# A new table of turns for a two-layer decoder kernel: every block of every stage gets a start of its own

## The reference, cut to what matters

```python
x = x + L0_attn(layernorm(x))        # Mamba-2: projection, causal conv, SSD scan in one chunk of 64, gate, projection
x = x + L0_xattn(layernorm(x), ctx)  # 16 heads over 64 context rows, with rotary tables on the keys
x = x + L0_ffn(layernorm(x))         # mixture of 7 experts, top 2, and a shared expert
x = x + L1_attn(layernorm(x))        # RWKV time mixing: scans with a running maximum
x = x + L1_xattn(layernorm(x), ctx)  # 32 query heads, 8 key/value heads, no projections
x = x + L1_ffn(layernorm(x))         # 64 small experts, top 8 by softmax, mapped by inv_map
```

## Time and profile before

| | |
|---|---|
| runs | 2320.09, 2321.63, 2322.1 us; median 2321.63 |
| profiled execution | 2316.73 us, of which the span is 2314.9 |
| busy | PE 2104.8 us (91%), DVE 1378.1 (60%), ACT 1003.4 (43%), POOL 687.6 (30%) |
| granted TensorE clock, mean | 0.957 |
| chain that ended last | PE 69%, DVE 14%, issue 7%, POOL 5%, DMA 2%, ACT 2% |

### The profile page before, as it was taken

The page is one execution under the profiler, slowest core; times in us unless marked ns, Lnnn a source line. Parts: engine busy times, 40 slices in busy tenths (PEclk is TensorE's granted clock), DMA queues, the critical chain, the costliest instruction groups (busy, mean ns, idle before and its releaser), DMA issues.

```text
span 2314.9 us, 37392 instructions
## 1 busy us (share of the span) xinstructions
PE 2104.8 (91%) x13552; PEld 1608.1 (69%) x13552; DVE 1378.1 (60%) x3477; ACT 1003.4 (43%) x1984; POOL 687.6 (30%) x1056
## 2 busy tenths in 40 slices
PE   5999999999999778999994569999999999999998
PEld 4888888888888556777772346666666666666655
DVE  3367777767766431233334567777777777777631
ACT  1245555555554322333331234455545445454542
POOL 1133333433433145111113333333332333323200
PEclk9799999999999879999997579999999999999999
DMA  6200050000000054222222000000000000000000
GB/s 192 72 3 21 8 176 24 8 17 24 8 8 15 5 186 143 62 69 73 70 69 105 10 19 24 24 24 24 22 24 24 24 24 24 24 24 24 15 5 7
DMA packets 80882, 99.67 MB, mean 43 GB/s; under 512 B 17976, under 2 KB 67008, under 8 KB 80192
## 3 DMA queue, kind: packets, MB, share of 16 engines
q1 hardware_dynamic: 74560, 80.49, 11.0%
q0 software_dynamic: 6144, 16.79, 2.2%
HBM read 62.12 MB, written 35.13 MB: 42 GB/s over the span
## 4 chain that ended last, share of the span: by engine, by line
PE 69%; DVE 14%; issue 7%; POOL 5%; DMA 2%; ACT 2%; SPq 0%; ACTq 0%; POOLq 0%; DVEq 0%
PE ps L1900 11%; PE ps L1315 8%; PE ps L348 6%; PE ps L748 5%; PE ps L707 5%; PE ps L1923 4%; PE ps L1906 3%; PE ps L718 3%; POOL rows_by_slot L1159 3%; PE ps L739 2%; PE ps L397 2%; DVE arena L1703 2%; DVE arena L1461 1%; PE ps L729 1%; PE ps L374 1%
## 5 line engine op out<-in xcount | busy, mean ns | idle before, releaser
L1900 PE MATMUL ps<-BIG,arena 128*128 128x352 f32 x512 | 166.9, 469 | 5.6 <-DVE arena L1990 5.6
L1900 PE MATMUL ps<-BIG,EARLY 128*128 128x352 f32 x512 | 165.9, 467 | 6.5 <-DVE EARLY L1990 6.5
L1315 PE MATMUL ps<-BIG,arena 128*128 x648 | 149.6, 383 | 13.7 <-POOL arena L1376 13.7
L348 PE MATMUL ps<-arena,EARLY 128*128 128x256 f32 x640 | 159.0, 393 | 0.7 <-DVE arena L450 0.7
L1349 DVE COPY arena<-ps 128x256 f32<-128x256 f32 x162 | 68.8, 424 | 137.1 <-PE ps L1315 137.1
L1315 PEld LDWEIGHTS ps<-BIG,arena 128*128 128x128 f32 x648 | 121.1, 190 | 34.8 <-issue 19.3
L1900 PEld LDWEIGHTS ps<-BIG,EARLY 128*128 128x128 f32 x512 | 92.8, 190 | 60.9 <-DVE EARLY L1990 12.2
L1900 PEld LDWEIGHTS ps<-BIG,arena 128*128 128x128 f32 x512 | 93.5, 191 | 59.2 <-DVE arena L1990 11.2
L348 PEld LDWEIGHTS ps<-arena,EARLY 128*128 128x128 f32 x640 | 121.0, 195 | 19.2 <-issue 2.9
L1367 ACT ACTIVATE arena<-ps,BIG 128x128 f32<-128x128 f32 x216 | 61.9, 369 | 117.7 <-PE ps L1306 106.3
L552 POOL TENSOR_TENSOR arena<-arena 128x512 f32<-128x512 f32 x32 | 40.6, 1270 | 242.1 <-DVE arena L477 242.1
(11 more groups left out here) (408 smaller groups left out, 5164.0 us busy)
## 6 DMA issues: line engine op xcount, KB each, us to landing
rows_by_slot<-zrow SPq DMA_DIRECT2D x5, 1792.0 KB, 15.4
arena<-rows_by_slot SPq DMA_DIRECT2D x54, 128.0 KB, 2.1
results_by_slot<-arena SPq DMA_DIRECT2D x54, 128.0 KB, 1.7
BIG<-in_moe_w SPq DMA_DIRECT2D x3, 1792.0 KB, 12.4
X<-in_x SPq DMA_DIRECT2D x8, 512.0 KB, 4.3
rows_by_token<-BIG SPq DMA_DIRECT2D x16, 256.0 KB, 2.2
EARLY<-rows_by_token SPq DMA_DIRECT2D x4, 1024.0 KB, 5.5
arena<-in_ka SPq DMA_DIRECT2D x16, 256.0 KB, 2.7
```

The costliest lines, as they stand in the source:

```text
L348: m = e.matmul(ps[:, f * 256:f * 256 + 256], w_in[:, c, c0 + f * P:c0 + f * P + P], L.hT[:, c, :], start=c == 0, stop=c == 1, skip_group_c ...
L1315: m = e.matmul(ps[:, 0:256], src[q][:, c * P:c * P + P], BIG[:, bass.ds(pe_reg[2 * n + q] + (w0 + c * 256), 256)], start=c == 0, stop=c == ...
L1900: e.matmul(ps[:, 0:352], L.hT[:, q, ts], WG[:, q, gs], start=q == 0, stop=False, skip_group_check=True)
```

## The change

Only the table changes: START gets a number for every block (before, blocks of a stage stood at one distance), and all of TURNS is new. No instruction is added or taken away, and no generator, wait, tile or ring is touched. `weave` now writes the same pieces in other orders: of the keys sorted, 986 of TensorE's 1515 pieces, 585 of VectorE's 1185, 666 of ScalarE's 1214, 133 of GpSimd's 490 and 110 of SyncE's 188 stand at another place, none further than 25 places off. The core of the diff:

```diff
-START = {"s1": line(0, 44.89, 16), "s2": line(75.9, 44.89, 16), "s3": line(167.3, 44.89, 16), "prod": [3, 6, 20, 26],
-         "first": [0], "x": [0, 37.9, 127.7, 217.5, 307.3, 397, 486.8, 576.6], "tables": [868.1], "scatter": [868.1,
-         890.1, 912.1, 934.1], "shared": line(868.3, 6.96, 16), "experts": line(958.1, 7.81, 35), "s4": line(1252,
-         60.03, 16), "s5": line(1311.7, 60.03, 16), "s6": line(1377.2, 60.03, 16), "ffn": [1253], "moe": [1.5]}
+START = {"s1": [-1.99, 40.46, 93.27, 139.51, 185.14, 231.83, 277.49, 323.58, 369.17, 416.8, 462.71, 508.88, 555.3,
+         601.65, 646.99, 693.28], "s2": [80.59, 127.61, 172.86, 218.49, 264.04, 310.66, 356.9, 403.43, 449.48, 495.3,
+         542.18, 589.47, 635.23, 680.78, 726.64, 772.92], "s3": [174.88, 231.57, 268.62, 314.54, 366.24, 404.42,
+         461.64, 499.36, 543.41, 589.39, 640.41, 684.8, 732.06, 777.5, 827.7, 865.48], "prod": [5.01, 18.55, 38.35,
+         55.95], "first": [13.33], "x": [-268.76, -154.84, -133.99, -123.44, -13.29, 118.5, 229.35, 355.66], "tables":
+         [936.28], "scatter": [832.51, 865.81, 869.14, 934.68], "shared": [912.61, 914.68, 922.23, 932.96, 944.26,
+         954.17, 956.39, 970.81, 970.95, 982.26, 987.09, 1052.88, 1053.31, 1056.92, 1134.49, 1138.18], "experts":
+         [1084.03, 1085.28, 1085.63, 1085.71, 1168.86, 1169.99, 1181.65, 1183.5, 1196.5, 1201.76, 1206.98, 1215.06,
+         1223.9, 1228.05, 1233.36, 1246.27, 1255.42, 1259.21, 1262.8, 1275.99, 1280.74, 1292.66, 1293.66, 1306.01,
+         1309.86, 1319.04, 1322.26, 1331.79, 1342.42, 1346.21, 1348.7, 1361.96, 1369.39, 1371.31, 1375.05], "s4":
+         [1413.94, 1733.48, 1844.57, 1905.29, 1966.59, 2028.25, 2090.45, 2151.8, 2213.22, 2274.44, 2335.33, 2397.56,
+         2458.67, 2519.3, 2581.96, 2643.31], "s5": [1734.41, 1844.33, 1905.23, 1966.73, 2027.86, 2089.94, 2151.09,
+         2213.08, 2274.41, 2335.67, 2397.16, 2458.03, 2519.87, 2581.46, 2643.22, 2703.75], "s6": [1849.18, 1910.39,
+         1971.83, 2033.3, 2095.17, 2156.41, 2217.76, 2279.59, 2340.85, 2402.32, 2463.73, 2525.2, 2586.66, 2647.88,
+         2708.78, 2767.71], "ffn": [1702.96], "moe": [1.5]}
 TURNS = {
-    "s1": {"dve": (0, 7.4, 35, 37.7, 46.3, 51.9, 62.4, 64.1, 66.3, 68.9, 72.3, 76.2, 79.1, 86.9),
...
-           "pe": (31.1, 33.8, 35.6, 39.7, 44.7, 50.1, 54.2, 59.7, 61.9, 62.2, 64.9, 65.8, 66.9, 70.6, 75.1, 76.4,
-            82.8),
...
+    "s1": {"dve": (3.69, 10.45, 33.14, 38.98, 46.66, 55.35, 65, 67.35, 68.38, 69.71, 70.9, 74.19, 79.19, 88.15),
...
+           "pe": (30.15, 32.92, 36.9, 43.63, 46.52, 51.24, 55.68, 61.5, 67.83, 67.83, 68.54, 71.16, 71.16, 71.83,
+            76.2, 78.23, 85.37),
...
+    "s2": {"sp": (-61.98,),
...
+    "prod": {"sp": (-107.75,),
+             "pe": (32.81, 39.21, 42.57, 47.73),
...
+    "x": {"sp": (87.52,)},
...
+    "scatter": {"sp": (33.6,),
+                "pool": (122.7,)},
+    "shared": {"sp": (-68.88,),
+               "pe": (1.75, 4.72, 10.07, 15.42, 21.39),
+               "act": (15.28, 21.1, 28.01),
+               "dve": (9.24, 13.45, 21.59)},
+    "experts": {"sp": (-6.75, 17.99),
+                "pe": (22.05, 24.4, 27.93, 31.38, 35.32, 39.85),
+                "act": (10.94, 18.07, 26.29),
+                "dve": (6.84, 13.22, 22.08),
+                "pool": (18.11,)},
...
+    "ffn": {"sp": (-282.01,),
+            "dve": (-30.94, -30.86, -30.37, -18.36, 11.56, 60.05, 98, 139.71, 139.71),
+            "pe": (-92.69, -92.69, -92.69, -53.84, -21.24, -20.66, 20.45, 29.25)},
```

More of the change, by code:

```diff
@@ new lines @@
+TURNS = {
+    "s1": {"dve": (3.69, 10.45, 33.14, 38.98, 46.66, 55.35, 65, 67.35, 68.38, 69.71, 70.9, 74.19, 79.19, 88.15),
+           "pool": (9, 16.41, 57.29, 58.39, 69.23, 73.25),
+           "pe": (30.15, 32.92, 36.9, 43.63, 46.52, 51.24, 55.68, 61.5, 67.83, 67.83, 68.54, 71.16, 71.16, 71.83,
+            76.2, 78.23, 85.37),
+           "act": (37.26, 44.56, 45.46, 52.63, 52.63, 60.09, 64.65, 68.34, 69.46, 69.56, 72.23)},
+    "s2": {"sp": (-61.98,),
+           "dve": (11.61, 15.29, 31.69, 35.91, 38.62, 42.66, 49.74, 57.38, 63.24, 66.36, 70.41, 90.6),
+           "pool": (4.35, 6.4, 37.47, 44.77, 60.29, 69.49),
+           "act": (17.15, 22.58, 25.59, 31.88, 32.41, 32.41, 35.69, 41.51, 49.73, 50.88, 51.27, 52.17, 55.9, 73.83,
+            74.97, 81.22, 83.1),
+           "pe": (19.3, 20.69, 28.37, 28.37, 28.37, 34.15, 34.15, 37.74, 46.26, 47.61, 54.18, 57.62, 62.48, 63.94,
+            70.76, 78.3, 81.81, 87.7)},
+    "s3": {"dve": (0.1, 21.23, 35.35),
+           "pool": (-3.9,),
+           "act": (4.04, 15.81, 31.73),
+           "sp": (-47.11,),
+           "pe": (9.44, 20.42)},
+    "prod": {"sp": (-107.75,),
+             "pe": (32.81, 39.21, 42.57, 47.73),
+             "dve": (38.8, 42.54, 46.21),
+             "act": (49.33,)},
+    "first": {"pool": (29.54, 75.98),
+              "sp": (-121.08,),
+              "act": (-161.65,),
+              "dve": (-6.67, 11.04)},
+    "x": {"sp": (87.52,)},
+    "tables": {"pe": (-23.17,),
+               "pool": (-32.79,),
+               "dve": (-21.16,)},
+    "scatter": {"sp": (33.6,),
[9 more added lines that the diff above has]
+                "pool": (18.11,)},
+    "s4": {"pool": (-7.01, 14.99, 14.99, 20.35, 20.94, 20.94, 22.49, 40.77, 40.77, 40.77),
+           "dve": (8.01, 25.44, 25.48, 26.92, 31.85, 39.37, 46.08, 55.1, 60.06),
+           "act": (16.13, 21.37, 25.64, 30.83, 36.73, 36.73, 37.45),
+           "pe": (21.29, 29.34, 31.9, 31.9, 58.04)},
+    "s5": {"sp": (-244.27,),
+           "dve": (4.28, 6.49, 18.93, 20.27, 27.64, 28.32, 57.9, 62.6),
+           "pool": (1.43, 5.31, 51.2, 59.24),
+           "pe": (10.76, 11.4, 16.74, 21.87, 24.59, 40.03, 42.26, 45.22, 47.81, 50.57, 54.87, 64.97),
+           "act": (12.73, 13.41, 22.21, 40.5, 41.36, 41.36, 49.49, 52.95, 54.89, 62.01)},
+    "s6": {"dve": (0.53, 9.48, 10.71, 20.2, 24.52, 31.57, 35.73, 43.83, 48.51, 49.21, 53.23, 64.97, 67.14, 76.81,
+            77.35, 82.91, 99.63),
+           "pool": (4.15,),
+           "act": (1.47, 3.51, 11.08, 26.43, 42.1, 46.44, 53.2, 55.06, 59.68, 59.68, 60.04, 64.77, 76.63, 77.47,
+            80.31, 85.02, 85.02, 85.34),
+           "pe": (3.26, 7.01, 16.56, 20.1, 35.27, 35.76, 42.09, 43.37, 48.52, 53.83, 59.01, 59.01, 61.46, 64.11,
+            72.26, 75.11, 78.55, 83.54, 86.65, 86.65, 91.98),
+           "sp": (172.39, 193.15)},
+    "ffn": {"sp": (-282.01,),
+            "dve": (-30.94, -30.86, -30.37, -18.36, 11.56, 60.05, 98, 139.71, 139.71),
+            "pe": (-92.69, -92.69, -92.69, -53.84, -21.24, -20.66, 20.45, 29.25)},
```

56 lines of the change are left out of this document (removed).

## The result

| | before | after |
|---|---|---|
| median (range) of the runs, us | 2320.86 (2318.1 to 2322.1) | 2254.27 (2244.93 to 2265.12) |
| ratio, 95% interval | | 0.9716 (0.9664 to 0.9769) |
| profiled execution, us (span) | 2316.73 (2314.9) | 2247.82 (2246.0) |
| busy, us | PE 2104.8, ACT 1003.4 | PE 2087.3, ACT 974.1 |
| granted clock, mean | 0.957 | 0.967 |

What follows compares the result with a forecast made beforehand. TensorE was taken as the bound, busy 2104.78 of 2314.9 us. Terms −22 + 3 − 3 + 0 − 11 − 3 − 7 = −43 from 2316.7 gave 2273.7, plus 4.9 about 2279 us; range 2262 to 2304.

Steps and rivals of the forecast that it cites:

- Start, −22: Start of the kernel: earlier statistics, covered weight loads of prod(2) and a higher TensorE clock save 22 us.
- 3.5 + 6.6 + 15.5: Start: shorter wait at L326 (3.5), no stall at L591 (6.6), full clock from 50 to 90 us (15.5).
- Stages 1 to 3, 0 in sum: Stages 1 to 3: +3 for small new waits, −3 at the end of stage 2 and ahead of s3(14).0.
- The costs of irregular blocks (+3, up to +20): Stages 1 to 3: blocks now differ, so small waits may appear, 0 to +20, taken as 3 for thirteen blocks.
- Mixture and shared expert, 0: Mixture and shared expert: earlier shared loads cut L1193's wait, but GpSimd's scatter chain stays; −6 to +8, taken as 0.
- Experts, −11: Experts: L1315's waits for GpSimd's product go (−16), +3 to +5 comes back; −14 to −3, taken as −11.
- Handover, −3: From experts to stage 4: L1405 ahead of the ffn products gains 7.1, about 4 comes back; −10 to +6.
- The +4 that I let come back: Handover: later L1426, VectorE and GpSimd pieces standing later, and a colder array cost together about 4 us.
- Stages 4 to 6, −7: Steady blocks of stages 4 to 6: L1610 and L1900 covered, 1.7 gained less 1.2 new waits, −0.5 for 13 blocks.
- my slower rival: Stage 4's single buffer set forms a ring, lengthened by the later s4.7: blocks 3.3 us longer, 2332 us; chance 0.06.
- Tail, 0: End of the kernel: no change, within 2 us either way.
- The rival "more", 2258: Array stays at full clock across the handover (12), start gains 27, steady blocks −1 each: 2258 us; chance 0.06.

Runs made afterwards that it cites:

- the pair without stalls: Kernel before and changed kernel, each without 12 of the 16 indirect DMAs of every scatter: 394.0 and 373.4 us from L1063 to the end of the last expert.
- f1: The changed kernel itself, unchanged, run again beside the kernel before on one chip: ratio 0.9692, median 2256.03 us.
- f3: The changed kernel with the mixture, the shared expert and the first eight experts back in the old order: ratio 0.9704 to before, median 2256.91 us.

## Why the prediction was wrong

The kernel was forecast faster, and it is; the mechanisms of the start, the experts and the handover's head hold. The size was off: 66 us for 42. The steps that failed are terms of the sum. In stages 4 to 6 the waits were counted at 1.7 us a block where they are 2.6, and the ramp into them (3.8) and the tail (5) stood at nothing without a reason. The 4 us that the handover was to give back never came. And the mixture stood at 0 because a chain of scatters was taken for its bound. In eighteen profiles the parts can be put beside each other free of single executions:

- **Start, −22; measured −25 (typical).** The sum of the parts was 25.6 (3.5 + 6.6 + 15.5), and I took 22 for a weight load that would still show. None does. All three steps are in the trace: L338 at 13.98 (forecast 13.6), no wait at L603, the clock 0.94 and 1.00. In the two profiles they give 3.1, 6.6 and some 16, close to the 25.6; the rest of the −31.6 is L683's 3.8, which I named and didn't count, L397's 1.1 and L348's 0.7. Part of the 31.6 is chance: the first L683 of the old order came at 89.7 to 103.3 in ten executions (mean 97.2), and the profiled one is the latest, with a long stretch of low clock; in the new order it came at 70.7 to 74.9 in seven (mean 72.1). That −22 came so near to −25 is in part luck: the step on the clock had one execution to go by.
- **Stages 1 to 3, 0 in sum; measured −4 to −5 of idle time behind the new start.** The costs of irregular blocks (+3, up to +20) don't exist: all ten windows from 116 to 696 have 58.00 of 58 busy. The gain is at the edges, as the −3 had it: in the two profiles the waits of L962 for L843 (6.1 to 4.1), of L729 for L933 (5.3 to 2.3) and of L397 (2.1 to 0) get shorter, and small ones come back. The 14 table loads less are there (ScalarE: 156 to 142 loads, L875's from 28 of the earlier trace rows to 14) and they could bring nothing in the windows in which TensorE is busy 58.00 of 58 in either order. The Trainium skill, "ScalarE: Activation LUTs", section "What ACT_TABLE_LOAD costs", puts a switch at about 2.66 us with its drain. The load alone is 1.283 us here; whatever the whole costs ScalarE, TensorE doesn't pay it in those windows.
- **Mixture and shared expert, 0; measured −12 in the pair without stalls, about −8 by the traces with them (16.4 less 8.6, below), 1 to 3 by the times of f1 and f3.** The size stays open; the step failed all the same. I argued from the earlier trace rows that the chain of scatters bounds the stage, since the experts' load follows the last scatter by 2.4 us. But TensorE still had three blocks of the shared expert to do at that time and was busy with them, so what it lost earlier at L1193 (14.3, and 5.1 more into other buffers) wasn't hidden. The new order loads those rows before the first scatter's: the wait falls to 0.9. The gaps of 7 and 6 us before shared(11) and the experts that I feared aren't there: without stalls, TensorE's longest wait behind L1063 is 1.2.
- **Experts, −11; measured −8.6 for the 27 from expert 8 on**, which would be 11 for 35. Right, by its own steps: 16 us less for GpSimd, and waits for ScalarE (L1327 for L1368 and L1379, 5.5) and of 3.3 to 4.6 us with no named cause come back.
- **Both together, in executions with those stalls:** from L1063 to the last expert 419.7 to 436.9 us in the old order (nine executions, mean 428.0) and 404.6 to 418.0 in the new (four, mean 411.6), −16.4; without stalls −20.6. The table's −4.5 compares an execution without stalls (before) with one that had them.
- **Handover, −3; measured −7.5.** L1405's −7.1 came out as −7.3. The +4 that I let come back is nothing. One sentence was plainly wrong: the ffn products don't move into the hole ahead of L1426, they stand behind it (TensorE's order lists s4(0).4 first). The array's clock stays low: from the end of the last expert to the first L1854 it is 0.67, where it was 0.66. That they could stand in the hole changes nothing, as the run showed.
- **Stages 4 to 6, −7; measured −12.6.** Two terms were mis-sized. I counted 1.7 a block gained, L1610 and L1900; L1923 (7.0 in twelve blocks) and L1416 (4.2) wait too, in all 31.5 us in twelve blocks, 2.6 a block. In the changed kernel 20 us remain, 1.7 a block:

```profile
PE ps L1876 <- DVE X L2007: 5.4, 11, 0.5
PE ps L1428 <- DVE arena L1715: 4.7, 10, 0.8
PE ps L1935 <- issue: 2.9, 8, 0.4
PE ps L1866 <- ACT arena L855: 2.5, 6, 0.6
PE ps L1866 <- ACT EARLY L855: 2.3, 6, 0.4
```

  and the period falls by 0.73, not 0.5. And the ramp: the third block took 64.5 before and takes 60.7, 3.8 that I had not looked for. L1854's slack of 0.79 is used up, and 0.4 beyond it is waited. The step that TensorE's order covers both waits was true only with ScalarE's order beside it; alone it costs 5.3 us a block, more than the 2.6 from which my slower rival decides. That rival named the lateness of s4.7 on VectorE, which is real (1.1 a block in the kernel without TensorE's order) but small; the large danger lay between TensorE and ScalarE.
- **Tail, 0; measured −5.** The last two blocks have waits too, and I gave them no term: TensorE's idle time behind the last L1405 falls from 12.4 to 8.0, 1.5 of it L1610's two waits.

The four misses after the start have one sign, and I had counted what could come back at each place and only the waits that I had rows of. The rival "more", 2258, had nearly the right size by luck: its reason, the clock across the handover, did not occur, and its sum takes 4 for half a us in 13 blocks, which is 6.5.

## What to carry to other kernels

A new order is to be judged as a set: what TensorE's order gains only holds if the engines that feed it have the matching order, and half of it can be slower than none. Take the whole list of the bounding engine's waits in a stage, not the largest two, and ask of a chain that seems to bound a stage whether the bounding engine has finished its own work when that chain ends. Where one part of a kernel scatters between executions, profile both kernels more than once before sizing that part.
